# A vision layer on one core: weight preparation on other engines, other first transfers, a new order of work on three engines

## The reference, cut to what matters

```
gray  = 0.2989 R + 0.587 G + 0.114 B
h     = (|conv3x3(gray, scharr_x)| + |conv3x3(gray, scharr_y)|) / 2
n     = layernorm(h)                       # over the last axis
ns    = n shifted by one row
k,v,r = ((n*tm + ns*(1-tm)) @ W.T)         # one tm and one W each
wkv   = running softmax-like mean of v over the rows, with decay exp(w) and bonus u (numerator, denominator)
h     = h + (sigmoid(r) * wkv) @ Wo.T
x2    = layernorm(h);  xhat = layernorm(x2)
e     = argmax(x2 @ Wg.T)                  # one of 8 experts for each row
h     = h + (gelu((xhat*scale_e + bias_e) @ W1_e + b1_e) @ W2_e + b2_e)
```

## Time and profile before

| | |
|---|---|
| runs | 1135.93, 1137.72, 1137.79 us |
| profiled execution | 1137.39 us, its span 1135.8 us |
| mean granted TensorE clock | 0.975 of full speed |
| busy: TensorE, VectorE, ScalarE, GpSimd | 1076.8, 1037.1, 972.2, 246.5 us |

### The profile page before, as it was taken

How to read it: one execution, slowest core, us unless ns; L and a number is a source line. 1 busy time by engine, 2 the same in 40 slices (tenths; PEclk the granted TensorE clock), 3 DMA queues, 4 the chain that set the end, 5 groups by cost and what they waited for, 6 DMA issues and landing times.

```text
span 1135.8 us, 17713 instructions
## 1 busy us (share of the span) xinstructions
PE 1076.8 (95%) x6107; PEld 776.8 (68%) x6107; DVE 1037.1 (91%) x1888; ACT 972.2 (86%) x1567; POOL 246.5 (22%) x291
## 2 busy tenths in 40 slices
PE   8656999999999999999999999999999999999986
PEld 3343677777777777777777777777777777777664
DVE  3879999999999999999999999999999999999820
ACT  1377899999999999999999999999999999998752
POOL 3111222212122222121122221221222212210001
PEclk9678899999999999999999999999999999999998
DMA  9668779898899899998988899989888999772223
GB/s 205 133 121 156 120 138 171 171 184 156 152 169 169 156 165 173 185 165 159 163 160 161 158 174 178 171 158 159 162 162 162 170 172 175 121 122 38 38 38 38
DMA packets 177777, 168.31 MB, mean 148 GB/s; under 512 B 14353, under 2 KB 177743, under 8 KB 177743
## 3 DMA queue, kind: packets, MB, share of 16 engines
q1 hardware_dynamic: 123784, 117.65, 47.9%
q0 software_dynamic: 50048, 48.25, 32.7%
q10 hardware_dynamic: 3910, 1.97, 1.0%
HBM read 102.80 MB, written 80.76 MB: 162 GB/s over the span
## 4 chain that ended last, share of the span: by engine, by line
ACT 60%; PE 31%; DVE 6%; issue 2%; POOLq 0%; POOL 0%; DVEq 0%; ACTq 0%
PE bank L1216 12%; PE bank L1253 9%; ACT hidden L1034 7%; ACT normed L1060 5%; ACT normed L941 5%; ACT bonus L1006 3%; ACT L1034 3%; ACT L1138 3%; ACT decay L993 3%; ACT part_v_hi L928 3%; ACT den L949 3%; ACT decay L987 3%; ACT fresh L998 3%; ACT fresh L982 3%; ACT v_sb L977 3%; ACT normed_t L1085 2%
## 5 line engine op out<-in xcount | busy, mean ns | idle before, releaser
L1377 PE MATMUL bank<-w_sb,hidden 128*128 128x256 f32 x1024 | 238.9, 380 | 1.9 <-ACT hidden L1034 1.9
L444 POOL DMA_DIRECT2D out_dram<-moe x64 | 77.1, 1299 | 627.9 <-ACT moe L1045 627.1
L1377 PEld LDWEIGHTS bank<-w_sb,hidden 128*128 128x128 f32 x1024 | 184.6, 190 | 30.3 <-ACT hidden L1034 2.7
L1310 PE MATMUL bank<-w_o_t,den 128*128 128x256 f32 x512 | 122.5, 393 | 5.1 <-DVE den L668 4.7
L1310 PEld LDWEIGHTS bank<-w_o_t,den 128*128 128x128 f32 x512 | 96.8, 194 | 43.8 <-ACT hidden L968 15.1
L1324 PE MATMUL bank<-normed_hi,w_hi 128*128 128x512 f32 x256 | 110.7, 432 | 1.9 <-DVE normed_lo L661 1.9
L1253 PE MATMUL bank<-rows_in,conv_w 102*32 102x512 f32 x960 | 109.4, 595 | 0.7 <-DVE gap L627 0.7
L1324 PE MATMUL bank<-normed_lo,w_hi 128*128 128x512 f32 x256 | 101.6, 397 | 0.0
L1324 PE MATMUL bank<-normed_hi,w_lo 128*128 128x512 f32 x256 | 101.3, 396 | 0.0
L599 DVE SCALAR_TENSOR_TENSOR mixed_vr<-normed,params,normed_t 128x512 f32<-128x512 f32 x128 | 89.5, 740 | 0.0
L1034 ACT ACTIVATE hidden<-bank,b_full 128x512 f32<-128x512 f32 x128 | 81.0, 696 | 4.8 <-PE bank L1346 3.8
(11 more groups left out here) (163 smaller groups left out, 2683.7 us busy)
## 6 DMA issues: line engine op xcount, KB each, us to landing
rows_in<-gray_dram SPq DMA_DIRECT2D x180, 256.0 KB
planes<-in_x_dram SPq DMA_DIRECT2D x120, 256.0 KB, 8.2
gray_dram<-planes POOLq DMA_DIRECT2D x120, 256.0 KB, 5.9
out_dram<-resid SPq DMA_DIRECT2D x64, 256.0 KB, 4.8
out_dram<-moe POOLq DMA_DIRECT2D x64, 256.0 KB, 6.3
gray_dram<-in_x_dram SPq DMA_DIRECT2D x60, 256.0 KB, 4.4
rows_in<-gray_dram SPq DMA_DIRECT2D x120, 24.0 KB
rows_in<-in_x_dram SPq DMA_DIRECT2D x6, 256.0 KB
```

Source lines behind the costliest of these rows:

```text
L444: pool.dma_start(out_rows(at.j, at.u - FFN, half), moe[:, 2 * half:2 * half + 2, :], accum_op=ALU.add).then_inc(added[half], 16)
L1310: ins = pe.matmul(bank[BANK_WO[half]][:, i * D:(i + 1) * D], rwkv[:, 2 * kt + i, half * P:(half + 1) * P], w_t[3][:, kt, :], start=(kt == ...
L1377: pe.matmul(ps, hidden[:, m, i, rows], w2_sb[:, m, :], start=(m == 0), stop=False)
```

## The change

Preparation: ScalarE copies the transposed weights, the parameters and the biases out of the banks, GpSimd makes the high and low parts, the convolution's weights, the split first layer and the parts of b2, all ahead of its step 0, except b2, ahead of its step 4. VectorE keeps two small operations (`setup_rates`). TensorE waits for GpSimd's split weights just ahead of its first `project_k(0)`. The buffers for the copied weights are separate, so the three don't wait for each other.

Transfers: Wk and Wv go ahead of pair 1's colours; the second image's colours of pair 1, the taps and the borders go from ScalarE's queue to SP's.

Order: all three lists change.

```
# SP, before step 0
 load_colors(sp, 0, 0)
-load_colors(sp, 1, 0)
 ... Wk, Wv
+load_colors(sp, 1, 0)
+load_colors(sp, 1, 1)
+... five loads of taps (scharr_dj); wait for the zeros; two borders of gray_dram   (all from ScalarE's queue)

# GpSimd
+def split_projections():
+    for i in range(3):
+        pool.wait_ge(s_act_setup, ACT_WEIGHTS + i)
+        prepared(pool.tensor_copy(w_hi[i][:, :, :], w_t[i][:, :, :]))
+        prepared(pool.tensor_tensor(w_lo[i][:, :, :], w_t[i][:, :, :], w_hi[i][:, :, :].bitcast(F32), ALU.subtract))
+def build_conv():          # 1 + 2 + 2 x (2 + 1) small operations on 102 partitions x 32 or 64
+def split_first_layer():   # waits for W1; two products of 128x512, a cast and a difference of 128x1024
+def split_b2():            # waits for b2; seven operations of 256 columns
-run_steps(pool, step)
+split_projections()
+build_conv()
+split_first_layer()
+run_steps(pool, step, {4: split_b2})
```

```
# ScalarE
+def setup_weights(at):     # step 2: parameters (wait for TensorE), exp(w), three copies of 128x512 from the banks
+def setup_experts(at):     # step 3: Wo (128x512), the router's weights, eight biases b1
 def log_denominator: -wait for s_den
 def fresh_arg:       +wait for s_gap[1]
 def fresh_of:        +wait for s_fresh_arg
 def bonus_of:        wait for s_rwkv of the pair before, in place of s_gap[1]
 def copy_normed2_high(ct): +wait for s_normed2_ps[1] where ct == 1
 def gelu(m):         the wait for the mask at m == 1 in place of m == 0

 step before                    step after
 scaled(0)                      scaled(0)
 copy_logits                    scaled(1)
 scaled(1)                      copy_logits
 copy_normed2_high(1, FFN)      high_r
 reciprocal                     log_denominator(PROJ)
 high_r                         reciprocal
 absolute(3), (2), (1), (0)     absolute(1)
 copy_v(0)                      copy_v(0)
 bonus_of                       absolute(2)
 fresh_arg                      fresh_arg
 decay_arg                      absolute(0), (3)
 decay_of                       setup_weights
 fresh_of                       copy_route
 reciprocal_std(0)              fresh_of
 copy_route                     bonus_of
 normalise                      decay_arg
 decay_rate (setup)             decay_of
 reciprocal_std(1)              reciprocal_std(0)
 gelu(0)                        normalise
 copy_v(1)                      copy_v(1)
 gelu(2), (1), (3)              reciprocal_std(1)
 normalise2                     gelu(1), (2), (3), (0)
 copy_normed(1), (0)            copy_normed(0), (1)
 gate_of(1), (0)                gate_of(0)
 table load                     normalise2
 log_denominator(WKV)           gate_of(1)
 high_k                         table load
 copy_normed2(0)                high_k
 high_v                         copy_normed2(0)
 copy_normed2(1)                copy_experts(0)
 copy_experts(0)                high_v
 copy_normed2_high(0)           copy_normed2_high(1)
 copy_experts(1)                copy_normed2(1)
                                copy_normed2_high(0)
                                copy_experts(1)
                                setup_experts
```

More of the change, by code:

```diff
@@ L595, in mix @@
+                assert own[0] == SETUP_RATES
             def mix(i):
@@ L1002, in bonus_of @@
                     return
-                wait(act, s_gap[1], at.count(stage, 1, 1))
+                wait(act, s_rwkv, at.count(stage, 1, 1, back=1))
                 for ct in range(CH):
@@ L1106, in step @@
                 scaled(0, GRAY, at)
+                scaled(1, GRAY, at)
                 copy_logits(FFN, at)
-                scaled(1, GRAY, at)
-                copy_normed2_high(1, FFN, at)
+                high_r(WKV, at)
+                log_denominator(PROJ, at)
                 reciprocal(PROJ, at)
-                high_r(WKV, at)
+                absolute(1, EDGE, at)
+                copy_v(0, WKV, at)
+                absolute(2, EDGE, at)
+                fresh_arg(WKV, at)
+                absolute(0, EDGE, at)
@@ L1371, in second_layer @@
                 if half == 0:
-                    wait(pe, s_hidden[3], at.count(stage, 1, 1))
+                    wait(pe, s_hidden[0], at.count(stage, 1, 1))
+                elif half == 1:
+                    wait(pe, s_gate[1], at.count(stage, 1, 1, back=-2))
                 for i in range(2):
```

321 lines of the change are left out of this document (160 added, 161 removed).

## The result

The changed kernel takes 1141.52 us, the median of 9 runs (1138.34 to 1142.44); the kernel before, measured beside it, 1136.38 (1134.68 to 1137.81). The ratio is 1.0035, interval [1.0023, 1.0048]: slower by 0.35% (the medians alone stand 0.45% apart). The forecast was 1144.5, which is 7.1 us (0.6%) over its base of 1137.4: the sign is right, the size too large. The nine runs fall into two groups, 1138.34 to 1140.0 at a mean granted clock of 0.981 and 1141.52 to 1142.44 at 0.978; the profiled execution, 1140.0 us with a span of 1138.4, is of the first.

The account below looks back on a forecast made before the run. It took a ring of ScalarE (23.44) and TensorE (8.84), 32.28 us a step, as the bound; 1137.4 + 14.6 (steady steps) - 5 (fill) - 2.5 (drain) = 1144.5 us, 8 in 10 from 1129 to 1151.

Parts of the forecast that it names:

- the first ring: Steady step: TensorE from routing product to transposes, then ScalarE back to the routing product; 32.80 us a step, +14.6 over 28.
- The second ring: Steady step: absolute value to routing product to last convolution, the old ring with passes moved in and out; 32.56 us.
- the 0.3 of the shift: Steady step, second ring: `normalise` directly follows `reciprocal_std(0)` and waits for VectorE's shift; 0.3 us.
- VectorE follows either ring: Steady step: VectorE has 31.6 us of work a step, so its moves cost nothing while the step is longer.
- The fill, -5: Start of the run: weight work leaves VectorE's path in two places; gain 5 us, bounds 0 and 7.5.
- the 4.69 of `setup_rest`: Fill: the last weights on VectorE, directly ahead of a running maximum on which the rest of that step hangs; 4.69 us.
- The 0.8 at the first place: Fill, first pairs: difference of `normed` no longer behind the preparation, 1.4 us, less about 0.6 for an added pass.
- The half microsecond for GpSimd and VectorE: Fill: cost of GpSimd's passes and VectorE's two-input passes excluding each other; half a microsecond.
- The drain, -2.5: End of the run: last step gains about 1.9, the two steps ahead lose and gain about 1 each; -1 to -4.
- TensorE did not set the step: Rival, steady step: ScalarE's part under 8.4 us, no wait at the routing product, step 31.89, 1119 us; chance 0.09.
- the rings were not shorter than 32.55: Rival, steady step: rings near 32.3 to 32.55 because passes overlap more; 1130 to 1137.5 us; chance 0.2.
- GpSimd blocked VectorE: Rival, fill: GpSimd late or blocking VectorE, fill gains nothing or loses a few; 1149.5 to 1153 us; chance 0.13.

Follow-up runs that it names:

- e1: ScalarE copies the second half of normed2 directly behind the first, against the changed kernel; 1137.6 us, 1.0016 of the kernel before.
- e7: e1 with ScalarE's copy of the transposed logits ahead of the two scalings of the colour planes; 1137.8 us, 1.0008 of the kernel before.
- e9: e7 with VectorE's second low part of normed2, best logit and hits earlier, and ScalarE's high_r behind the denominator's reciprocal; 1137.4 us, 1.0003 of before.
- e12: Kernel before with its three old orders, plus the new preparation on ScalarE and GpSimd and new transfer order; 1136.6 us, 0.9991 of before.
- e6: Changed kernel with GpSimd splitting the first layer's weights later, behind its first gray turn; 1138.9 us, 1.0020 of the kernel before.
- e10: e9 with GpSimd splitting the first layer's weights behind its first gray turn; 1136.4 us, 0.9996 of the kernel before.

## Why the prediction was right in sign and too large

The step of the prediction that made the size too large is the sum of the first ring, 32.80 for 32.67. The drain gained more than was booked as well; the fill erred the other way.

- **The steady step, +14.6, measured +10.7.** The ring was there, level with a second, where the forecast had it 0.24 ahead. Its terms were each a little long: TensorE 22.79, measured 22.71; to the copy 0.67 (a row of the fill), measured 0.64; ScalarE 9.34, measured 9.32. Together 32.80 against 32.67, and 28 x 0.13 is 3.6 us. The second ring, summed at 32.56, came out at 32.67: its chain goes over the output projection and VectorE's statistics and shift, of which only the 0.3 of the shift was booked. That it came out level with the first to a few hundredths is chance.
- **"VectorE follows either ring; its moves cost nothing while the step is above that."** Wrong, though it did not show in the sum. A full engine that waits 1.1 a step for `high_k` and then runs 17 to 19 us without a hole is part of a ring of its own, and that one stood at 32.5. It is why e1, e7 and e9 could not get the 0.69 back.
- **The fill, -5, measured -2.0 and -3.1 in two profiles.** The term that failed is the 4.69 of `setup_rest`, taken as wholly on the path. Its removal brought the running maximum 3.93 forward and the end of that step 1.95 (e12). The named successor, "the projections and convolutions on TensorE, at about the same time", was there; its price was not taken off. The 0.8 at the first place did not come either: the difference of `normed` started at 37.65 in place of 36.64, waiting for ScalarE's copy, behind a first convolution that had started 1.30 later. The half microsecond for GpSimd and VectorE was too little: 4.5 us of longer passes, worth 1.0 to 2.0 in the fill (e6 against two profiles; 0.7 in e10 against e9). The transfers, taken as 0, cost about 0.45, within the scatter.
- **The drain, -2.5, measured -6.1.** At like clock up to the last routing product -2.8 to -3.6, and about 1.5 of that is a higher clock in the last step, so the work alone is worth between 1 and 2. The term of 1.9 for the last step measured about 1.5 at like clock. The rest came from the granted clock, which no sum of instructions holds; that 2.8 lies near the 2.5 booked is in part luck.
- **The rivals and signs.** TensorE did not set the step; the rings were not shorter than 32.55; GpSimd blocked VectorE in the way described, as longer passes and not as idle time, but the fill still gained. The waits came as named. The chain of waits crossed to ScalarE at `normalise`, not at the copy of `normed`, and the last absolute value of the sixth step came at 123.73 and 122.68, not at about 121. In the profiled execution the three differences add up: 1144.5 - 3.9 (step) + 3.0 (fill) - 3.6 (drain) = 1140.0. With both fills and the drain at like clock they are 10.7 - 2.0 to 3.1 - 2.8 to 3.6, which is 4.0 to 5.9 us; the ratio says 4.0, interval 2.6 to 5.5.

## What to carry to other kernels

Where three engines are all nearly full, list every ring that closes over a wait, VectorE's too, and add each up to the hundredth: a cut in one gives only the distance to the next. Before an edit is costed by what it takes off an engine, follow the work behind it to the next engine that is late, at the clock which that engine will have after its wait. When preparation moves to GpSimd, put it where VectorE does not run passes of two tiles.

## What was not expected of the hardware

- GpSimd and VectorE lengthened each other: VectorE's passes of two tiles from 1.22 to 2.07, and two of 1.41 together to 4.19, GpSimd's cast of 128x1024 from 1.04 (e6) to 1.91; VectorE's statistics, reading one tile, stayed at 1.41.
- The same work behind step 33 took 100.0 or 103.3 us with the granted clock (1.00 or 0.96 up to the last routing product); that alone is 0.3% of the run, as much as the whole effect of the change.
